# First attention of a gated cross-attention kernel: slot transfers by six, the maxima's bounce in two pieces, their transpose in bank 5

## What is computed

```python
x = x + jnp.tanh(g_xattn[0]) * _L0_xattn_ref(_layernorm(x, axis=-1), ctx_1024, ...)
x = x + jnp.tanh(g_ffn[0]) * _L0_ffn_ref(_layernorm(x, axis=-1), ...)
x = x + jnp.tanh(g_xattn[1]) * _L1_xattn_ref(_layernorm(x, axis=-1), ctx_1024, mask_BxS2_bf1, ...)
x = x + jnp.tanh(g_ffn[1]) * _L1_ffn_ref(_layernorm(x, axis=-1), ...)
```

```python
q = _ln((x @ Wq + bq).reshape(b, s1, H, HD), qn_w, qn_b)
k = _ln(kv[..., :HD], kn_w, kn_b)
k_dca = _ln(kv_dca[:, :, 0], kn_dca_w, kn_dca_b)
ctx = _attn(qT, k.transpose(0, 2, 1, 3), v.transpose(0, 2, 1, 3))
ctx_dca = _attn(qT, k_dca.transpose(0, 2, 1, 3), v_dca.transpose(0, 2, 1, 3))
return (ctx + DCA_WEIGHT * ctx_dca) @ Wo + bo
```

## Time and profile before

| | |
|---|---|
| median of 3 runs | 1687.81 us (1685.54 to 1689.53) |
| profiled execution | 1685.9 us |
| its span | 1684.5 us |
| PE, DVE, ACT, POOL busy in the span | 86%, 73%, 67%, 47% |
| mean granted clock of TensorE | 0.942 |
| first attention | from the start to about 578 us |

### The profile page before, as it was taken

One profiled execution on the slowest core, in us unless ns is written; L12 is line 12 of the kernel. 1 busy time (PEld: TensorE's weight loads), 2 busy tenths in 40 slices (PEclk: granted clock), 3 DMA queues, 4 the chain that ended last, 5 costly groups with the idle time before them and its releaser, 6 DMA issues.

```text
span 1684.5 us, 25330 instructions
## 1 busy us (share of the span) xinstructions
PE 1454.9 (86%) x8374; PEld 711.7 (42%) x8460; DVE 1229.2 (73%) x2184; ACT 1127.1 (67%) x2020; POOL 792.1 (47%) x615
## 2 busy tenths in 40 slices
PE   5687988888888887688898989899899999999979
PEld 3243343343333343244444444344544455455445
DVE  6765766666686356478887768899589997788937
ACT  3567667667764755477787668678477775788724
POOL 3014013014030001078766749787486877577823
PEclk8798997897999999799999999999999999999989
DMA  4001200200340100100000100000000000000000
GB/s 154 1 1 39 43 1 11 50 1 1 60 176 1 51 1 5 39 21 6 1 1 23 38 20 6 26 1 1 6 26 1 26 1 1 1 1 1 1 1 26
DMA packets 20488, 36.69 MB, mean 22 GB/s; under 512 B 4898, under 2 KB 15238, under 8 KB 19334
## 3 DMA queue, kind: packets, MB, share of 16 engines
q1 hardware_dynamic: 20358, 35.07, 7.2%
HBM read 26.53 MB, written 1.15 MB: 16 GB/s over the span
## 4 chain that ended last, share of the span: by engine, by line
PE 35%; POOL 9%; issue 7%; DVE 5%; ACT 3%; POOLq 0%; DMA 0%; ACTq 0%; DVEq 0%; SPq 0%
PE BK L582 35%; POOL arena L1878 6%; DVE arena L1514 3%; DVE arena L1497 1%; ACT arena L1760 1%; ACT arena L1768 1%; POOL arena L1875 1%; POOL arena L1853 1%; ACT arena L1753 1%; POOL arena L1884 1%; POOL arena L1863 1%; DVE arena L886 0%; PE BK L866 0%; ACT L1753 0%; DVE arena L1528 0%
## 5 line engine op out<-in xcount | busy, mean ns | idle before, releaser
L582 PE MATMUL BK<-arena 128*128 128x512 bf16 (+10 forms) x8044 | 1407.2, 378 | 192.6 <-DVE arena L1497 30.6
L582 PEld LDWEIGHTS BK<-arena 128*128 128x128 bf16 (+7 forms) x8130 | 674.2, 115 | 894.8 <-issue 235.1
L1878 POOL TENSOR_TENSOR arena<-arena 128x512 f32<-128x512 f32 (+1 forms) x352 | 509.5, 1447 | 178.6 <-ACT arena L1753 154.5
L1514 DVE TENSOR_TENSOR arena<-arena 128x512 bf16<-128x512 f32 (+1 forms) x416 | 514.4, 1245 | 39.7 <-ACT arena L1760 38.8
L1753 ACT ACTIVATE arena<-BK,arena 128x512 f32<-128x512 f32 (+1 forms) x416 | 285.9, 687 | 132.3 <-PE BK L582 117.1
L1329 DVE TENSOR_REDUCE arena<-BK 128x1 f32<-128x512 f32 x384 | 244.0, 683 | 65.6 <-PE BK L582 64.4
L1661 ACT ACTIVATE arena<-BK 128x512 f32<-128x512 f32 (+1 forms) x416 | 226.0, 598 | 76.0 <-PE BK L582 69.6
L1760 ACT CAST arena<-arena 128x512 bf16<-128x512 f32 (+1 forms) x416 | 253.3, 609 | 0.0
L1768 ACT ACTIVATE arena<-BK 128x512 bf16<-128x512 f32 (+1 forms) x256 | 130.0, 508 | 87.8 <-PE BK L582 86.7
L1497 DVE CUSTOM_DVE_ANT_0 arena<-BK,arena 128x512 bf16<-128x512 f32 (+1 forms) x256 | 145.7, 569 | 47.4 <-PE BK L582 37.5
L1802 POOL TENSOR_TENSOR arena<-arena 128x256 f32<-128x256 f32 (+6 forms) x45 | 30.2, 671 | 208.1 <-ACT arena L1600 205.7
(11 more groups left out here) (170 smaller groups left out, 863.8 us busy)
## 6 DMA issues: line engine op xcount, KB each, us to landing
arena<-arena SPq DMA_DIRECT2D x144, 50.0 KB, 2.2
arena<-in_ctxT SPq DMA_DIRECT2D x8, 800.5 KB, 4.4
arena<-in_ctxk SPq DMA_DIRECT2D x4, 768.0 KB
arena<-in_wo SPq DMA_DIRECT2D x1, 2048.0 KB, 7.9
arena<-in_wqT SPq DMA_DIRECT2D x1, 2048.0 KB, 7.7
arena<-in_x SPq DMA_DIRECT2D x4, 256.0 KB, 11.0
arena<-in_rsel SPq DMA_DIRECT2D x1, 1024.0 KB, 9.2
arena<-in_rw1T SPq DMA_DIRECT2D x1, 1024.0 KB, 5.1
```

Of the source, the lines that this page charges most:

```text
L582: return T.matmul(out_, lhsT, rhs, start=start, stop=stop, skip_group_check=True)
L1514: V.tensor_tensor(Pl[k][0:m, :], P1[k][0:m, :], Ph[k][0:m, :], ALU.subtract).then_inc(p_low, 1)
L1878: G.tensor_tensor(acc[0:m, g % 2, :], acc[0:m, g % 2, :], P1[k][0:m, :], ALU.add).then_inc(summed1, 1)
```

## The change

- `kd` becomes four pieces of six DMAs for each half. Pieces 0 and 1 are put ahead of the two `qr`, piece 2 where `kd` was, piece 3 one yield later. The waits are the same.
- `mneg` goes to bank 5 and comes right at the yield behind `mm`; before, one yield was left empty between them. The writing to DRAM stays with `mneg`; the wait for its landing and the reading back become a piece `mrow` of their own, two yields later.
- A group of maxima has 30 yields and not 29; `pace` spreads 30 over the 26 half steps.

```diff
                 if b:
                     for p in (4 * hf, 4 * hf + 2):
+                        piece("kd", b, hf, p // 2 % 2)
                         piece("qr", b, p, bank=bank())
                         yield
-                    piece("kd", b, hf)
+                    piece("kd", b, hf, 2)
+                    yield
+                    piece("kd", b, hf, 3)
                     known.update((b, p) for p in range(4 * hf, 4 * hf + 4))
                     yield
...
             piece("mm", g)
             yield
-            yield
-            piece("mneg", g, bank=7)
+            piece("mneg", g, bank=5)
+            yield
+            yield
+            piece("mrow", g)
             rowed.add(g)
             yield
...
-            while paced[0] * 26 < (2 * (s + LEAD0) + half) * 29:
+            while paced[0] * 26 < (2 * (s + LEAD0) + half) * 30:
...
-                    T.transpose(BK[7][0:16, 0:128], mmx[:, g % 2, :], idn[:, :]).then_inc(full[7], 1)
+                    T.transpose(BK[i][0:16, 0:128], mmx[:, g % 2, :], idn[:, :]).then_inc(full[i], 1)
...
-                    V.tensor_scalar(mneg[:, g % 2, :], BK[7][0:16, 0:128], -1.0, None, ALU.mult).then_inc(free[7], 1)
+                    V.tensor_scalar(mneg[:, g % 2, :], BK[i][0:16, 0:128], -1.0, None, ALU.mult).then_inc(free[i], 1)
...
                 elif kind == "kd":
-                    b, hf_ = arg
+                    b, hf_, p = arg
...
-                    for p in range(4):
-                        for r in range(2):
-                            for k, src in enumerate((kth[hf_], ktl[hf_], kth[hf_])):
...
+                    for r in range(2):
+                        for k, src in enumerate((kth[hf_], ktl[hf_], kth[hf_])):
...
                 elif kind == "mneg":
...
                     SP.dma_start(rowd[k], mneg[:, k, :]).then_inc(bounced[k], 16)
+                elif kind == "mrow":
+                    g, = arg
+                    b, qd, k = g // 4, g % 4, g % 2
                     sp.wait_ge(bounced[k], 16 * (g // 2 + 1))
```

More of the change, by code:

```diff
@@ L1928, in sync_main @@
                         sp.wait_ge(*filled("sc", 52 * (b - 1) - 1, 1))
-                    for p in range(4):
-                        for r in range(2):
-                            for k, src in enumerate((kth[hf_], ktl[hf_], kth[hf_])):
-                                at, of = 64 * r + 16 * k, 32 * p + 16 * r
-                                SP.dma_start(kst[b % 2][at:at + 16, 4 * hf_ + p, :], src[of:of + 16, :]
-                                             ).then_inc(slotted[hf_], 16)
+                    for r in range(2):
+                        for k, src in enumerate((kth[hf_], ktl[hf_], kth[hf_])):
+                            at, of = 64 * r + 16 * k, 32 * p + 16 * r
+                            SP.dma_start(kst[b % 2][at:at + 16, 4 * hf_ + p, :], src[of:of + 16, :]
+                                         ).then_inc(slotted[hf_], 16)
                 elif kind == "mneg":
```

## The result

The changed kernel takes 1698.53 us (median of 18 runs, 1690.25 to 1704.80), the kernel before on the same chips 1687.95 us (18 runs, 1683.04 to 1692.01). The ratio is 1.0061, 95% interval 1.0045 to 1.0077: some 10 us slower. Neither the 1685.5 us nor the range up to 1690.5 held it.

A forecast was written before the change was run, and what follows sets the result against it. TensorE, busy 86% of the span, was taken as the bound, held up by SP's slot block and the transpose. Terms -3.3 + 1.0 + 0.8 - 0.8 = -2.3 us gave 1685.5 us against the 1687.8 median; range 1679.5 to 1690.5.

The forecast's parts named there:

- The pace: First attention, two groups where VectorE is full: 30 yields leave more half steps without a tile; 0.8 us lost.
- The transpose: Transpose of the maxima, first attention: in bank 5 and earlier it no longer waits for bank 7; 3.3 us gained.
- new wait: Transpose now arriving just as its last maximum does: 0.1 us in ten groups, 1.0 us lost, bounds 0 and 26.
- the 0.8 us put down to the clock: TensorE behind group 13's wait: part of a half-clock stretch comes back, 0.8 us gained, bounds 0 and 3.
- Slot pieces at 0: SP's slot transfers in sixes: the 48 still leave in one block in batches 2 and 3; 0 us.
- The way through DRAM at 0: Bounce and rows split on SP: two weight loads now precede group 13's rows; taken as 0, bounds 0 to 2 lost.
- Pinned waits for rows: TensorE at groups 7 and 11: SP's block fixes its restart, so two waits of 3.5 to 4.5 us stay.
- The slow rival: Transpose early for its maximum holds up scores and values: 6 us on top of the forecast, 1691.5 us, chance 0.14.
- The pieces do break the block: SP lets group 7's bounce through: both row waits, 7.7 us, and up to 5 more go; 1673 us, chance 0.03.

The follow-up runs named there:

- the fourth: The kernel with 28 yields and spread slot transfers, changed to put the final maximum right behind the second tail, giving 27 yields: 1661.33 us, 0.9844 to before.
- e5_28: Kernel before with the transpose in bank 5 and the reading back right behind the final maximum, 28 yields, pace 28: 0.9985 [0.9968, 1.0002].
- e13_short30: Kernel before with one more empty yield, pace 30, and tile maxima taken over 128 of 512 columns: 1670.65 us.
- e12_short29: Kernel before, at 29 yields, with tile maxima taken over 128 of 512 columns: 1658.18 us.

## Why the prediction was wrong

**The pace: the step that failed.** The prediction took 0.5 us a group for two groups, 0.8 us, because it counted only the steps left without a tile, and only where VectorE is full. It measured 12.5 us: (1.0061 - 0.9987) x 1688, and by itself in the kernel before the same, 0.0074 x 1689. Even its bound of 8 us, 0.5 in all sixteen groups, was too low. What the sum left out is the other side: the same 26 tiles in 22.5 half steps instead of 23.3 stand in a fourth pair in each group, and the tiles come to stand elsewhere among the other pieces. TensorE, which keeps its order, waits in front of a tile until VectorE has emptied its bank, with the scores that ScalarE needs behind it: 13.8 us more for the tile maxima and 11.1 us more for the exponentials. That the pace costs this is shown. Why the tiles are late is argued from the stalls; of the reasons at hand, the place ahead of scores was tried and gave nothing back, the time of a reduction is left open above, and neither the other work ahead of it on VectorE nor the order of TensorE's own pieces was tried. The prediction had this rule in hand for the transpose and did not put it to the tiles. The Trainium skill, TensorE: Matmul & The Clock Gate, Step-by-step: what each phase is for, cited there, has matmuls in program order; the 3.03 us in front of the matmuls at 520.39, and ScalarE's 3.88 us behind them, agree.

**The transpose.** 3.3 us gained less 1.0 of new wait were forecast. Bank 5 alone at the old place gave 3.2 us (0 to 6.2 by its interval). That this meets the 3.3 is partly luck, since 1.7 of them (groups 13 and 14) were to come from the earlier place, which that kernel hasn't. The wait for the last maximum was 2.55 us instead of 1.0. Right in kind; the net of the earlier place was not measured by itself, and neither were the 0.8 us put down to the clock.

**Slot pieces at 0.** The order of SP came out as read, with the block whole. Alone they measured 4.6 us faster, with 0.8 to 8.1 in the interval, so 0 was too low. What gave it is open: its two waits for rows are 0.45 and 1.87 us instead of 4.17 and 3.53, but its profile is 2.9 us of span above that of before, so shows no gain to follow.

**The way through DRAM at 0.** No row wait came at group 13: the loads left at 497.09 and 497.48, the rows at 497.97, and TensorE waited for nothing there. The two loads landed 3.1 and 4.2 us from issue. Right. It was not tried alone.

**Pinned waits for rows.** "One or two us earlier, 3.5 to 4.5 us left" is wrong: 1.08 us is left. They are pinned on SP's side only: how long TensorE stands there depends on when it arrives. Of the 7.7 us the pace alone leaves 5.1 (3.44 and 1.65) and the slot pieces alone, at 29 yields, 2.3, though from the block's start to TensorE's restart there are 36.4 and 35.3 us, close to the 35.6 and 35.8 of before. So the slot pieces, costed at 0, took more of these waits than the slower pace did. When 28 yields let TensorE come sooner, there are three (1.98, 3.51, 4.75). A slot block of 32 us is thus what a faster kernel runs into, and what hid the gain of 28 yields.

**Rivals.** The slow rival's mechanism (the transpose) hardly happened (2.55 us in seven of the sixteen groups); the kernel became slower in another way. "The pieces do break the block" did not happen in this change, but its price was about right: spread, they gave 10.1 us (0.994), where 7.7 and up to 5 were said.

## To carry to other kernels

In an order written by hand, a number that spreads work over slots ("30 over 26") is a change to every group: list where two pieces come to share a slot, and ask whether the in-order engine will stand in front of something another engine needs, and what work of the engine that frees the slot stands ahead of the piece. Try such a number apart from the edits it comes with: here it turned 2 us of gain into 10 of loss. And take away the waits that confound a series before reading its slope, then test the slope at one point outside; here it held for three kernels and not for the fourth. And read a shortened kernel in its trace as well as by its median: here the two disagreed on whether the shortening had taken the cost away. The version that beats both has 28 yields, the transpose in bank 5 right behind the final maximum, and the second half's slot transfers spread over the groups: 1662.05 us, 1.4% below the kernel before.

## What the runs showed of the hardware

Behind the wait of 3.51 us in e5_28, TensorE's granted clock was 0.50 for ten microseconds, and about as much time was lost again (30.12 against 26.24 us) as by the wait itself (24.78 against 20.88). This second part is uneven. Windows behind two such waits of e13_short30, of 5.73 us (the first) and 4.19 us (the last two):

```profile
316.00:319.00 3.00, 2.91 (x19) 0.72 (x19) 0.61 (x3) 1.08 (x2) 0.00 (x0) 0.50 0.00 0
319.00:323.00 4.00, 3.82 (x43) 1.34 (x45) 1.48 (x6) 2.79 (x6) 0.00 (x0) 0.79 0.00 0
...
447.00:451.00 4.00, 4.00 (x34) 1.17 (x31) 1.25 (x5) 2.17 (x4) 0.00 (x0) 0.50 0.00 0
451.00:455.00 4.00, 4.00 (x30) 1.46 (x24) 0.88 (x4) 1.67 (x3) 0.00 (x0) 0.50 0.00 0
```

Behind the longer wait the clock was back within seven microseconds, behind the shorter it was still at half after 10.7. Each of the longer stretches cost some 4 us against e12_short29, where it did not come. So a single profile can put two like kernels several microseconds apart.

A wait that a view gives to one line of VectorE is not that line's time: the 3.03 us given to L1334 hold 0.68 us of it, and 2.63 us are still given to it where it takes 0.29.
